# Turning a quad's pages two quads ahead of their gate matmuls in a fused cross-attention and mixture-of-experts kernel

## The reference

```python
x = x + cross_attention(layernorm(x), ctx)        # 16 heads of 8
t = layernorm(x).reshape(4096, 128)
shared = silu(t @ sg.T) * (t @ su.T) @ sd.T       # 128 wide, every token
scores = sigmoid(t @ gate_w.T) + gate_bias        # 64 experts in 8 groups
# the best 4 groups are kept; in them the best 6 experts, weights normalised to sum 1
h = silu(einsum('th,eih->eti', t, eg)) * einsum('th,eih->eti', t, eu)   # 64 wide
x = x + shared + einsum('eti,ehi,te->th', h, ed, comb)                  # comb: 6 weights a token
```

## Time and profile before

| | |
|---|---|
| time, median of 3 runs | 871.64 us (868.51 to 877.1) |
| span of the profiled execution | 860.9 us |
| median less that span | 10.7 us |
| TensorE matmul busy | 515.8 us (60%) |
| VectorE, GpSimd, ScalarE busy | 453.8, 389.5, 355.5 us |
| mean granted TensorE clock | 0.676 of full |
| page loop, first gate to last down | about 393 to 821 us |

### The profile page before, as it was taken

How to read it: one execution, slowest core, us unless ns; L and a number is a source line. 1 busy time by engine, 2 the same in 40 slices (tenths; PEclk the granted TensorE clock), 3 DMA queues, 4 the chain that set the end, 5 groups by cost and what they waited for, 6 DMA issues and landing times.

```text
span 860.9 us, 12037 instructions
## 1 busy us (share of the span) xinstructions
PE 515.8 (60%) x3204; PEld 433.7 (50%) x3204; DVE 453.8 (53%) x2264; ACT 355.5 (41%) x962; POOL 389.5 (45%) x425
## 2 busy tenths in 40 slices
PE   3877655554356654315897567476876767665700
PEld 2545443332234432205896567475775767665700
DVE  6486666555565756564153444365464654243452
ACT  3464433443433532212283454355554554234400
POOL 2006555555555565565205434343435435444464
PEclk9985555556755555556698676687868687778765
DMA  7333222222222232242363333244434444444231
GB/s 219 139 124 105 96 93 69 71 84 95 99 99 99 93 102 99 96 149 64 105 163 99 92 96 100 76 123 105 111 104 111 113 127 120 126 115 107 74 98 49
DMA packets 98708, 90.60 MB, mean 105 GB/s; under 512 B 10576, under 2 KB 85456, under 8 KB 98640
## 3 DMA queue, kind: packets, MB, share of 16 engines
q1 hardware_dynamic: 85232, 64.26, 25.3%
q0 software_dynamic: 12288, 25.29, 10.6%
q10 hardware_dynamic: 1120, 0.28, 0.1%
HBM read 41.32 MB, written 48.46 MB: 104 GB/s over the span
## 4 chain that ended last, share of the span: by engine, by line
PE 26%; issue 25%; POOL 22%; another core or an unknown queue 13%; ACT 9%; DVE 4%; ACTq 1%; POOLq 0%; DMA 0%; DVEq 0%
POOL pages L445 17%; PE bank_s L1141 14%; PE bank_q L1141 4%; PE bank_s L1137 3%; ACT d_now L497 2%; PE bank_o L1141 2%; ACT gu_now L497 2%; POOL rstd L435 2%; ACT pxt L497 1%; POOL p_t L478 1%; PE bank_r L1141 1%; ACTq L497 1%; POOL empty L478 1%; PE bank_w L1141 1%
## 5 line engine op out<-in xcount | busy, mean ns | idle before, releaser
L1141 PE MATMUL bank_s<-pxt,gu_now 128*128 128x64 f32 x768 | 124.7, 331 | 96.5 <-ACT pxt L497 75.0
L1141 PEld LDWEIGHTS bank_s<-pxt,gu_now 128*128 128x128 f32 x768 | 120.4, 246 | 101.7 <-ACT pxt L497 79.4
L478 POOL DMA_INDIRECT p_t<-results,place_i x96 | 91.2, 950 | 149.6 <-DVE xb L1081 69.6
L1097 DVE TENSOR_TENSOR h_t<-bank_s,s_act 64x256 f32<-64x256 f32 x128 | 54.7, 427 | 185.6 <-ACT s_act L658 107.0
L478 POOL DMA_INDIRECT empty<-results,place_i x96 | 90.9, 947 | 105.1 <-DVE xb L1081 58.6
L445 POOL DMA_INDIRECT pages<-payload,place_i x96 | 93.1, 970 | 38.5 <-issue 27.4
L445 POOL DMA_INDIRECT pages<-payload_b,place_i x96 | 93.1, 970 | 35.2 <-issue 26.4
L658 ACT ACTIVATE s_act<-bank_s 64x512 f32<-64x512 f32 x64 | 37.8, 591 | 132.1 <-remote 86.2
L435 POOL TENSOR_TENSOR rstd<-ve,minus_half 128x4 f32<-128x4 f32 (+1 forms) x21 | 18.5, 882 | 134.0 <-DVE ve L913 131.2
L519 ACT ACTIVATE p_t<-bank_s 128x512 f32<-128x512 f32 x64 | 36.1, 598 | 65.5 <-issue 26.9
L1241 PE MATMUL bank_o<-bias_h,row_h 96*128 96x256 bf16 x16 | 6.2, 388 | 76.1 <-ACT o_t L497 74.1
(11 more groups left out here) (169 smaller groups left out, 1164.6 us busy)
## 6 DMA issues: line engine op xcount, KB each, us to landing
pg<-pages SPq DMA_DIRECT2D x64, 258.0 KB
results<-y_s SPq DMA_DIRECT2D x64, 256.0 KB
pages<-empty SPq DMA_DIRECT2D x21, 774.0 KB
w_gu<-in_expert_gu SPq DMA_DIRECT2D x16, 256.0 KB
w_d<-in_expert_d SPq DMA_DIRECT2D x31, 128.0 KB
out_x<-xb SPq DMA_DIRECT2D x16, 128.0 KB
xb<-in_x SPq DMA_DIRECT2D x3, 512.0 KB, 7.9
pages<-payload,place_i POOLq DMA_INDIRECT x96
```

Of the source, the lines that this page charges most:

```text
L478: pool.indirect_dma_start(out=ys[n % YS_SLOTS][:, k, :], out_offset=None, in_=results[0:landed * QUAD * P, :], in_offset=bass.IndirectOffs ...
L1097: dve.tensor_tensor(h_t[q % 2][h * INTER:(h + 1) * INTER, :, h, :], gu_ps[q % 2][INTER:2 * INTER, :].rearrange("p (g h t) -> p g h t", g=Q ...
L1141: return pe.matmul(dst, w, v, start=True, stop=True)
```

## The change

TensorE calls `page_x(q + 2)` where it called `page_x(q + 1)`, after `gate_up(q)`, and turns quads 0 and 1 ahead of the loop. ScalarE's copy to `pxt` moves in the same way: in `quad(q)` it copies quad q + 2, and quads 0 and 1 ahead of the loop. Buffers stay two each. Two waits are written in: TensorE's `page_x(q)` waits until ScalarE has copied quad q - 2 out of the same PSUM half, and ScalarE's copy waits until the gate of quad q - 2 has read the same `pxt` buffer. No work is added or removed.

```diff
@@ ScalarE
             def page_x(q):
                 act.wait_ge(pxt_done, q + 1)
+                if q >= 2:
+                    act.wait_ge(gu_done, q - 1)
                 copy(pxt[q % 2][:, :], xt_ps[q % 2]).then_inc(pxt_ready, 1)
...
-                if q + 1 < NQ:
-                    page_x(q + 1)
+                if q + 2 < NQ:
+                    page_x(q + 2)
...
             page_x(0)
+            page_x(1)
@@ TensorE
             def page_x(q):
                 j = q % SLOTS
                 pe.wait_ge(page_in[j], 16 * (q // SLOTS + 1))
+                if q >= 2:
+                    pe.wait_ge(pxt_ready, q - 1)
                 transposes([xt_ps[q % 2][:, g * P:(g + 1) * P] for g in range(QUAD)], [pg[j][:, g, 0:D] for g in range(QUAD)],
                            pxt_done)
...
             page_x(0)
+            page_x(1)
...
                 gate_up(q)
-                if q + 1 < NQ:
-                    page_x(q + 1)
+                if q + 2 < NQ:
+                    page_x(q + 2)
```

## The result

The changed kernel takes 831.72 us (median of 4 runs, 826.84 to 836.0) against 871.24 us of the kernel before (4 runs): a ratio of 0.9589, 95% interval 0.9512 to 0.9666, so 29 to 43 us less. The forecast was 838 us, with 804 to 872 as its range. Some executions of one kernel are over 1.5% slower than its fastest; the ratios of this document leave these out, so they differ a little from the quotients of the medians.

What follows compares the result with a forecast made beforehand. In the bursts, TensorE's finished work was taken to be reported late, after the burst's last DMA. Gains of 22, 10 and 2 us make 34: 860.9 - 34 = 827 us of span, plus 10.7 outside it, 838 us; range 804 to 872.

Steps and rivals of the forecast that it cites:

- the two regimes: Before the first gather ScalarE bounds, TensorE close behind; in the bursts, TensorE's results are reported late, after the last DMA.
- the dead time: In bursts, while a gate's signal is out: TensorE would run the next gate then, its SiLU following 3.55 us after the first.
- Ahead of the gathers: nothing: Before the first gather: no gain, as the copy stays in ScalarE's 3.55 us and TensorE's gaps are at most 1.15 us.
- The start, 2 us of at most 3.7: At the loop's start, gate 3 moves into idle time while scatters run: 2 us gained, bounds 0 and 3.7.
- Double bursts, 10 us: From 457 to 562 us, four bursts of twelve DMAs wait for stored results: 2.5 us gained on each, 10 us.
- Late stretch, 22 us: Between 575.00 and 812.75 us, ten long cycles become short, 2.2 us each: 22 us.
- the short kind: Late-stretch cycle with 4.6 to 5.6 us of GpSimd idle time before a burst; SiLU let through before the burst's last DMA.
- The long kind: Late-stretch cycle with 6.7 to 7.9 us of GpSimd idle time before a burst; its SiLU comes only at the release.
- more: Rival, chance 0.13: in every second late cycle the down's signal also precedes the hold; 34 us more gained, 804 us.
- The three terms: The forecast's gains: 22 us in the late stretch, 10 in the double bursts, 2 at the start; 34 us.
- Nothing: Rival, chance 0.22: TensorE is really busy in the gap, or running ahead only lengthens the held queue; 862 to 876 us.
- slower: Rival, chance 0.13: TensorE, more at the high clock, has each combine's SiLU held to the release; 880 to 905 us.

Runs made afterwards that it cites:

- e5: The kernel before without its gathers, combines adding whatever lies in the buffers: 679.46 us.
- e7: The changed kernel with each gather replaced by six plain DMAs of the same size from SyncE, from rows of x: 678.88 us, ratio 0.7875.
- e10: The changed kernel with each gate waiting again for the copy to pxt that follows the previous quad's SiLU: 871.92 us, ratio 1.0021 to before.
- e3: The kernel before with pages turned and copied two quads ahead only for quads 13 to 24, one ahead elsewhere: 854.5 us, ratio 0.9856.
- e4: The kernel before with pages turned and copied two quads ahead only from quad 25 on, one ahead elsewhere: 842.39 us, ratio 0.9694.
- e1: The changed kernel with each gate waiting again for ScalarE's SiLU of the quad before: 854.18 us, ratio 0.9752 to before.
- e11: The changed kernel with the last three DMAs of a gather also waiting for the SiLU of the quad after the combine: 821.76 us, ratio 0.9508.
- e13: The changed kernel with the last three DMAs of a gather waiting for the SiLU of the second quad after the combine: 802.45 us, ratio 0.9286.

## Why the prediction was right, and where it was not

**Bound and mechanism.** The reading of the two regimes held. Late signals come with the indirect DMAs that GpSimd issues (e5, e7), the change fills the dead time (most of a gate runs in it, the second SiLU 3.44 us after the first; forecast 3.55), and the wait of the gate for pxt is gone. What did not hold as it stands is "A hold is a matter of the high clock inside a burst; a gate at the low clock was passed on". The low-clock gate of the earlier trace rows that it was read from ran from 667.78 to 671.46, between two bursts, so it could not show this; and the downs at 605.19 and 667.48 above go against it. Counted over ten traces with gathers (all but e10's, from which gate records are missing), for the gates and downs that end inside a burst or up to 1.6 us after it, by the time from the burst's first DMA to the recorded end. "Late" is one whose reader, with nothing else to do on record, starts over 0.5 us after it, with no other engine named as the cause:

| end, us after the first DMA | high level | low level |
|---|---|---|
| 0 to 2 | 9 of 71 late | 2 of 49 late |
| 2 to 4 | 71 of 89 late | 4 of 41 late |
| 4 to 6 | 72 of 138 late | 19 of 32 late |

(In the last row of the high level the reader is often still behind an earlier late result, so more may be late than the count says.) So the place in the burst counts as well as the level, and the low level puts the lateness off and does not prevent it. Why is open.

**Ahead of the gathers: nothing.** Right to the resolution: TensorE is busy 34.00 of 34 us there, from 32.85, and from the SiLU of quad 4 to the first gather it is 28.9 us before (427.87 to 456.76) and 28.6 after (428.90 to 457.54).

**Two waits at no cost.** By program order both are met when they are reached: each asks for a count that the engine has just waited for (TensorE's gate for pxt_ready >= q + 1, ScalarE's SiLU for the gate of quad q). e10, which has both of them and one more, is at 1.0021 (0.9968 to 1.0075) of before: they cost nothing that can be measured.

**The start, 2 us of at most 3.7.** From the SiLU of quad 2 to the first gather there were 38.3 us before (418.45 in the earlier trace rows; the first gather at 456.76). After:

```profile
422.34 0.59 ACT L660 ACTIVATE s_act<-bank_s 64x512 f32<-64x512 f32 x1 [4.41 <-remote]
...
424.03 0.59 ACT L660 ACTIVATE s_act<-bank_s 64x512 f32<-64x512 f32 x1
...
457.54 0.98 POOL L478 DMA_INDIRECT p_t<-results,place_i  x1 [37.52 <-DMA results<-y_s]
```

35.2 us, so 3.1 us less, and the next SiLU follows after 1.69 us where it took 4.84 (418.45 to 423.29).

**Double bursts, 10 us.** The stage takes 97.9 us where it took 105.8, so 7.9 us; e3 says 5 to 20. It is not 2.5 us for each of four: the idle times behind the four double bursts were 9.8, 12.8, 9.9 and 14.4 us and are now 7.5, 9.9, 10.4 and 11.1, so three gain 2.3 to 3.3 us and one nothing.

**Late stretch, 22 us.** From there to ScalarE's last y_s copy, 821.80 before and 789.93 after: 259.2 against 234.5, so 24.7 us; e4 says 20 to 34. The size was right and the working was not. The step "So the next combine's SiLU comes ahead of the hold, and the cycle becomes the short kind, limited by the down's signal" failed. The long kind stayed, at 7.1 us of idle time, and the short kind fell from 5.6 to 2.6, in the direction of the rival "more". The timeline above shows what came in place of the forecast. The gate ahead of the combine did not end 1 to 2 us after the burst's first DMA but 4.1 us after (603.90 to 607.98), late enough to be held: TensorE reached it only behind a low-level gate (599.36 to 602.87) and down 31. And in the other cycle the down's signal was not held, so the combine ran inside the burst. That the right size came out is partly luck. The first eight cycles take 96.9 us (555.46 to 652.36) where they took 110.2 (562.60 to 672.81), a gain of 13.3 us that comes nearly all from the short kind. The other 11.4 us come from the rest of the stretch, where bursts join and no cycle is of either kind for long.

**Why "more" did not come on top.** Where both kinds might have been short, bursts joined: from 677.06 to 692.41 twelve DMAs run with one stop of 0.83 us, the SiLU waits 11.60 us to 694.30, and the next burst starts only at 703.43, after 11.02 us. There the twelve act as one long hold. That joining is what keeps the whole at the forecast's size is read from this one place and from the list of bursts; no run tests it.

**The credit to the dead time was too broad.** The forecast counted only a gate that runs while the signal is out. e1 keeps the SiLU in the chain, so no gate can run ahead of a late SiLU, and still gains 2.5%. A shorter chain after each release would do this; that it is this is argued, not shown.

**The constant outside the span was wrong, and cancels.** I took 10.7 us between the median and the profiled span. The runs now listed show 1.7 to 1.9 us between a run's span and its time (831.4 and 833.1), so the profiled execution of before took about 862.6 us, less than any of the four listed. The forecast is in effect the median less the sum, 871.6 - 34, so the constant does not move it. The sum is short of the gain of the medians, 39.5 us, and above that of the two profiled spans, 29.5; 34 lies inside the interval of 29 to 43.

**What the sum left out.** The three terms measure 3.1 + 7.9 + 24.7 = 35.7 us, and the profiled spans differ by 29.5. In the profile after, the SiLU of quad 2 comes 3.9 us later than before (422.34 against 418.45). That is not the change's doing as far as the traces show: in the variants it comes between 416.77 and 424.05, with pages one or two quads ahead. And from ScalarE's last y_s copy to the end it is 41.5 us, not 39.1, where the prediction has "The tail after the last down is set by the last four gathers and stays"; in the variants with gathers it is 37.8 to 40.6, so this is at most a small cost, and its cause is open.

**The rivals.** "Nothing" (the second rival; the prediction calls it the third) is out by the time. Of its two readings, that TensorE's recorded ends are models and too early finds no support in e5 and e7, where with the same matmuls no SiLU waits on "remote"; in the bursts it is bounded only by the 1.3 us worked out above. Of "slower" the mechanism is there: TensorE at the higher clock (0.83 against 0.77) is held in each long cycle and stopped inside its gates, but the time that its waits without a releaser take is no more than before (32.9 against 35.6 us).

## What to carry to other kernels

When a consumer starts microseconds after its producer's recorded end, look at what another engine issues in that time before blaming the producer, and replace that issue by plain DMAs of the same size to see whether it is the cause. Work that needs no answer from the held engine can be moved into the gap by one more stage of run-ahead, with the buffers that are there, if program order already keeps them apart. Test such a change by putting back the exact chain, all of its links: half of it gave a number between both theories.

## What the runs showed of the hardware

What TensorE finishes while GpSimd issues indirect DMAs can reach the others late. Little of what ends in the first 2 us of a burst is late (11 of 120 gates and downs in ten traces). From 2 to 4 us most of the high level's results are (71 of 89) and few of the low level's (4 of 41); from 4 to 6 us the low level's are too (19 of 32). Where they are held to the end of a burst, they are let through 1.5 us after its last DMA in the timeline above (611.11 to 612.61), and in the ten traces mostly 1.4 to 1.7 us after it behind six DMAs, 2.0 to 2.1 behind nine in a row (e11, e13) and 2.3 to 2.7 behind twelve (before, the copy of a down's result starts at 474.00 and the last DMA ends at 471.51). Others are let through inside a burst. TensorE itself then also stops between matmuls (611.08, 612.52); in the joined bursts its gate goes on by one matmul in 1.4 us (684.26, 685.69, 687.14, 688.58, 690.01, 691.43). The same bytes by plain DMAs from SyncE, at clock 1.00 and DMA share 0.72, make nothing late. Not issuing the indirect gathers is worth 21% of this kernel, some 20 us of it behind the loop (from the last y_s copy to the end 18.7 us in e5, 39.1 before); issuing them at other moments brought 3%.
